# A graph-network kernel: the PE's signals in weighted, maximum and convolution passes moved from matmuls to one drain per unit

## What is computed

```
msg = relu(h_in[src] + edge_attr @ We[l] + be[l])          # L0, five message layers
agg = segment_sum(msg, dst)
...
agg = segment_sum(x[src] * edge_weight, dst)               # L1, the weighted pass
...
amax = segment_max(leaky_relu(a_src[src] + a_dst[dst]), dst)   # L2, the maximum pass
out  = segment_sum(h[src] * exp(alpha - amax) / denom, dst)    # L2, the attend pass
...
h = segment_sum(h[src] * norm, dst)                        # L3, three convolution passes
```

## Time and profile before

| | us |
|---|---|
| median of 3 runs | 10497.17 |
| lowest, highest | 10493.28, 10524.75 |
| the profiled execution | 10512.7 |
| its span, from the first to the last instruction | 10510.6 |

### The profile page before, as it was taken

The page is one execution under the profiler, slowest core; times in us unless marked ns, Lnnn a source line. Parts: engine busy times, 40 slices in busy tenths (PEclk is TensorE's granted clock), DMA queues, the critical chain, the costliest instruction groups (busy, mean ns, idle before and its releaser), DMA issues. The chain is left out here.

```text
span 10510.6 us, 129336 instructions
## 1 busy us (share of the span) xinstructions
PE 6092.0 (58%) x27369; PEld 4863.8 (46%) x27370; DVE 4112.3 (39%) x9347; ACT 1787.8 (17%) x5309; POOL 5218.2 (50%) x5246
## 2 busy tenths in 40 slices
PE   3567666765675666667456533457854564455454
PEld 2456545644563555456334423345633443344343
DVE  5344434444453444434312523337761223224123
ACT  3222222222222222222323210001210000000000
POOL 2654454445446545644565445530036655655655
PEclk9788877877887888778778865558977787788777
DMA  5332332333233323323322145423313222222322
GB/s 149 108 94 86 98 102 84 98 90 103 83 93 103 96 85 98 105 84 89 92 82 79 32 138 165 148 97 131 114 60 88 83 71 86 85 80 72 87 78 70
DMA packets 423906, 995.27 MB, mean 95 GB/s; under 512 B 124608, under 2 KB 190016, under 8 KB 407360
## 3 DMA queue, kind: packets, MB, share of 16 engines
q0 software_dynamic: 246800, 677.71, 22.4%
q1 hardware_dynamic: 152608, 293.79, 8.5%
q10 hardware_dynamic: 24336, 22.16, 0.6%
HBM read 858.93 MB, written 134.35 MB: 95 GB/s over the span
## 5 line engine op out<-in xcount | busy, mean ns | idle before, releaser
L283 POOL DMA_INDIRECT ring<-node_table,idx x4608 | 4510.2, 979 | 3679.3 <-issue 1667.8
L250 DVE SCALAR_TENSOR_TENSOR S<-iota,block_start,dst_f 128x512 f32<-128x512 f32 x1900 | 1423.2, 749 | 3256.2 <-remote 1813.2
L497 PE MATMUL psAT<-ring,S 128*128 128x256 f32 x7600 | 2023.4, 426 | 1065.6 <-DVE AGG L614 917.8
L321 PE MATMUL psAT<-ring,S 128*128 128x256 f32 x6080 | 1709.1, 443 | 1506.2 <-DVE AGG L365 743.3
L497 PEld LDWEIGHTS psAT<-ring,S 128*128 128x128 f32 x7600 | 1599.8, 216 | 1424.0 <-DVE S L250 759.9
L321 PEld LDWEIGHTS psAT<-ring,S 128*128 128x128 f32 x6080 | 1332.8, 225 | 1878.1 <-issue 1024.0
L656 DVE TENSOR_TENSOR ring<-ring,psE 128x256 f32<-128x256 f32 x2560 | 877.0, 416 | 744.7 <-remote 358.2
L566 ACT ACTIVATE ring<-ring 128x256 f32<-128x256 f32 x2560 | 841.9, 408 | 1235.0 <-issue 651.4
L283 POOL DMA_INDIRECT ring<-att_table,idx x512 | 492.6, 962 | 471.3 <-issue 471.3
L438 PE MATMUL psE<-we_stk,stk 128*128 128x256 bf16 x2560 | 428.5, 307 | 308.4 <-DVE ring L656 156.7
L750 PE MATMUL psAT<-shared,S 128*128 128x9 f32 x1520 | 340.1, 363 | 393.1 <-DVE shared L796 310.6
(11 more groups left out here) (304 smaller groups left out, 4772.8 us busy)
## 6 DMA issues: line engine op xcount, KB each, us to landing
stk<-stack_table SPq DMA_DIRECT2D x320, 256.0 KB
ring<-node_table,idx POOLq DMA_INDIRECT x4608
rows_table<-ring SPq DMA_DIRECT2D x64, 1072.0 KB
ring<-rows_table SPq DMA_DIRECT2D x64, 1072.0 KB, 4.9
node_table<-tab ACTq DMA_DIRECT2D x136, 128.0 KB
stack_table<-stk SPq DMA_DIRECT2D x64, 256.0 KB, 2.0
node_table<-tab SPq DMA_DIRECT2D x96, 128.0 KB, 1.7
ring<-att_table,idx POOLq DMA_INDIRECT x512
```

What stands on the lines that cost most here:

```text
L250: nc.vector.scalar_tensor_tensor(S[:, 4 * g:4 * g + 4, :], iota[:, :].unsqueeze(1).to_broadcast([P, 4, P]), block_start[:, bass.ds(blk, 1) ...
L283: nc.gpsimd.indirect_dma_start(ring[:, q, 0:gw], None, table, bass.IndirectOffsetOnAxis(ap=idx[:, q:q + 1], axis=0)).then_inc(gathered[q], 16)
L321: ins = nc.tensor.matmul(psA[:, 0:D], S[:, u, :], ring[:, q, 0:D], start=(u == 0), stop=(u == U - 1))
L497: ins = nc.tensor.matmul(psA[:, 0:D], S[:, u, :], ring[:, U * ob + u, 0:D], start=(u == 0), stop=(u == U - 1))
```

## The change

In `edge_pass`, `max_pass` and the side work of the weighted pass no matmul or transpose carries a signal any more. After the 8 matmuls of a unit the PE drains, and the drain adds 8 to `onehot_used`. The drain at the end of an octet goes, and `octet_free` is raised by a plain semaphore instruction. In `max_pass` a drain signals `scoresT` and another one `runsT`. The start of the weighted pass (`turn_weights`) and its side work do the same. `message_pass`, `attend_pass` and the node phases stay as they were.

```diff
@@ edge_pass, the unit
-                                    ins = nc.tensor.matmul(psA[:, 0:D], S[:, u, :], ring[:, q, 0:D],
-                                                           start=(u == 0), stop=(u == U - 1))
-                                    if u % 4 == 3:
-                                        ins.then_inc(onehot_used, 4)
+                                    nc.tensor.matmul(psA[:, 0:D], S[:, u, :], ring[:, q, 0:D],
+                                                     start=(u == 0), stop=(u == U - 1))
+                                pe.drain().then_inc(onehot_used, U)
                                 pe.reg_add(npe, npe, U)
 
                             units(pe, None, cnt, unit)
-                            pe.drain().then_inc(octet_free, 1)
+                            pe.sem_inc(octet_free, 1)
@@ max_pass
-                            nc.tensor.transpose(psE[:, 512:512 + P], d16[:, :], ident[:, :]).then_inc(scoresT, 1)
+                            nc.tensor.transpose(psE[:, 512:512 + P], d16[:, :], ident[:, :])
+                            pe.drain().then_inc(scoresT, 1)
...
-                            nc.tensor.transpose(psE[:, 1536:1536 + P], last[:, :], ident[:, :]).then_inc(runsT, 1)
+                            nc.tensor.transpose(psE[:, 1536:1536 + P], last[:, :], ident[:, :])
+                            pe.drain().then_inc(runsT, 1)
...
-                                        if u % 4 == 3:
-                                            ins.then_inc(onehot_used, 4)
+                                    pe.drain().then_inc(onehot_used, U)
@@ turn_weights, root_pe
-            ins.then_inc(weights_turned, 1)
+            pe.drain().then_inc(weights_turned, 1)
...
-                ins.then_inc(root_turned, 1)
+                pe.drain().then_inc(root_turned, 1)
...
-                ins.then_inc(root_done, 1)
+                pe.drain().then_inc(root_done, 1)
```

More of the change, by code:

```diff
@@ L749, in unit @@
                                             pe.wait_ge(onehot_ready, c + u + 4)
-                                        ins = nc.tensor.matmul(psA[:, (HEADS + 1) * u:(HEADS + 1) * (u + 1)],
-                                                               S[:, u, :], picks[:, U * half + u, :],
-                                                               start=True, stop=True)
-                                        if u % 4 == 3:
-                                            ins.then_inc(onehot_used, 4)
+                                        nc.tensor.matmul(psA[:, (HEADS + 1) * u:(HEADS + 1) * (u + 1)],
+                                                         S[:, u, :], picks[:, U * half + u, :],
+                                                         start=True, stop=True)
+                                    pe.drain().then_inc(onehot_used, U)
                                     pe.reg_add(npe, npe, U)
@@ L1851, in turn_weights @@
                     for g in range(2):
-                        ins = nc.tensor.transpose(turned_weight(s_, f)[:, P * g:P * g + P],
-                                                  w1_sb[:, g, D * s_ + P * f:D * s_ + P * f + P], ident[:, :])
-            ins.then_inc(weights_turned, 1)
+                        nc.tensor.transpose(turned_weight(s_, f)[:, P * g:P * g + P],
+                                            w1_sb[:, g, D * s_ + P * f:D * s_ + P * f + P], ident[:, :])
+            pe.drain().then_inc(weights_turned, 1)
         def copy_weights(dve):
@@ L1878, in root_pe @@
                     for f in range(2):
-                        ins = nc.tensor.transpose(psT[:, D * q + P * f:D * q + P * f + P],
-                                                  tin[:, q, P * f:P * f + P], ident[:, :])
-                ins.then_inc(root_turned, 1)
+                        nc.tensor.transpose(psT[:, D * q + P * f:D * q + P * f + P],
+                                            tin[:, q, P * f:P * f + P], ident[:, :])
+                pe.drain().then_inc(root_turned, 1)
             if ob == 2:
@@ L1887, in root_pe @@
                     for f in range(2):
-                        ins = nc.tensor.matmul(psO[:, D * q:D * q + D], tT[:, q, P * f:P * f + P], wb_sb[:, f, :],
-                                               start=(f == 0), stop=(f == 1))
-                ins.then_inc(root_done, 1)
+                        nc.tensor.matmul(psO[:, D * q:D * q + D], tT[:, q, P * f:P * f + P], wb_sb[:, f, :],
+                                         start=(f == 0), stop=(f == 1))
+                pe.drain().then_inc(root_done, 1)
         def root_act(act, i, ob):
```

## The result

| | before | after |
|---|---|---|
| median of 4 runs, taken together, us | 10510.96 | 10633.86 |
| lowest, highest | 10493.28, 10528.30 | 10602.67, 10670.11 |
| span of the profiled execution | 10510.6 | 10668.0 |
| mean granted TensorE clock | 0.783 | 0.783 |

The ratio is 1.0122, with a 95% interval of 1.0085 to 1.0159. A repeat on another chip, `change_again`, gave 1.0108 (1.0073 to 1.0142).

A forecast was written before the change was run, and what follows sets the result against it. It took POOL's gather stream, interrupted by PE's late signals, to bound the passes. Gains of 457 + 40 + 235 = 732 us from 10512.7 gave 9780.7, or 9770 as median; range 9600 to 10,700, for its own case 9600 to 10,000.

The forecast's parts named there:

- I take the first: PE's drains: lateness taken at its lower bound, the shortest old drain, 0.22 us in all.
- it is signals on matmuls that queue for a passage: PE's signals during POOL's gathers: they pass one at a time, and the old drain was late standing behind one.
- The upper bound: PE's drains: a drain is as late as the matmul signals are in the old kernel.
- 732 us of gain: Whole kernel: 457 from POOL's waits in edge passes, 40 at pass ends, 235 in the maximum pass.
- The stretch of the earlier trace that I gave as proof: Convolution pass: two pending signals came 6 us apart, the octet's drain at once after; POOL resumed 0.7 us after DVE.
- POOL's own stop lets them through: Passes with gathers: PE's signals arrive late while POOL streams gathers and get through when POOL stands still.
- not touched: Message layers, where POOL waits 996 us, the attend pass and node phases: left out of the gain.
- POOL's floor: Passes with gathers: 512 gathers at 1.25 us cannot take less than 640 us.
- rival 1: Edge and maximum passes: drains as late as signals, nothing gained, later one-hots added; 10,650 to 10,750 us, chance 0.27.
- The later one-hot: DVE's first half of S moves behind the unit's last matmul: +0.75 us per unit, +0.4 between octets, +0.9 in maximum pass.
- they come out during DVE's 1.3 us of one-hot and add: PE's branch and waits behind a unit's drain in edge passes: hidden by DVE's work, so no cost.
- The swap of the octet's drain: Octet's end in edge passes: a semaphore instruction replaces the drain at the same place, costed at nothing.

The follow-up runs named there:

- wait_landing: Kernel before, but POOL waits after each octet for its last gather to land, in weighted, maximum and convolution passes; 10402.62 us, ratio 0.9918.
- edge_drain: Kernel before with the change in the weighted and three convolution passes alone; 10582.66 us, ratio 1.0066.
- bare_drain: Kernel before, both signals kept, plus a drain that carries nothing behind each unit of the edge and maximum passes; 10591.93 us, ratio 1.0076.
- one_signal: Kernel before with a unit's two signals merged onto its 8th matmul in edge and maximum passes, no drain added; 10559.02 us, ratio 1.0051.
- max_drain: Kernel before with the drain per unit in the maximum pass alone, scoresT and runsT still signalled on matmuls; 10579.53 us, ratio 1.0067.
- drain_and_landing: Changed kernel, but POOL waits after each octet for its last gather to land, in weighted, maximum and convolution passes; 10389.72 us, ratio 0.9906.

## Why the prediction was wrong

**The step that failed** is "I take the first", the choice of the lower bound for a drain's lateness, with its reason, "it is signals on matmuls that queue for a passage". The upper bound was the true value: drains without a signal ahead of them took up to 33.6 and 40.2 us. All of the 732 us of gain hung on it. The stretch of the earlier trace rows that I gave as proof bears the other reading as well: if matmuls retire in order and late, the drain always follows right after the last one, however it was held. It could not tell the two apart, and I let it weigh against the old drains, which were often late (107 of 256). The 6 us between two signals were no queue either: in the stretch at 6499 us of the same trace, shown above, three signals that were held come out within 0.13 us. The Trainium skill (PSUM — Partial Sum Buffer, "Engine vs sequencer instructions") says that a drain waits until the engine is fully idle. These traces agree: each of the changed kernel's 475 unit drains ends behind its unit's last matmul record, by 0.02 to 38.2 us.

**What held.** On a chip with holds POOL's stream is what goes with the lateness, and a full stop after each octet removes it: `wait_landing` shows it. That "POOL's own stop lets them through" is true of most long holds, not of all (83 of 92, above). The message layers kept their length, but "not touched" hid that they lose most: with the stops everywhere a layer falls from 963 to 983 us to 851 to 868. That POOL's floor bounds the passes once PE is prompt was also right: 656 to 674 us for 512 gathers without holds, where I had computed 640.

**The terms of rival 1.** The later one-hot was priced at 0.75 within an octet and at most 0.4 at its end; the medians are 0.66 and 0.37, and the edge passes lost 90 us in the trace and 73 in `edge_drain`, against 93. The maximum pass was priced at 63 x 0.9 = 57; it measured 59 in the unit matmuls. That both sums came out near the measured ones, with a wrong make-up, is luck. I costed PE's sequencer behind the drain at nothing, "they come out during DVE's 1.3 us of one-hot and add", and the step to the next pair not at all. `bare_drain` measured +82 for that, and `one_signal` +50 for what I thought was all. The cover is there only within an octet; at the end of an octet the drain now stands ahead of the loop's branch (+0.37 in `bare_drain`), and before the next pair it keeps PE from running ahead (+1.08). On the other side the late one-hot costs less than priced; my explanation, which no run tests, is that a unit that is held loses nothing by it.

**The swap of the octet's drain** for a plain increment "at nothing" took the octet's end alone; the drain that stands there now, ahead of the loop's branch, is the +0.37 above. The side work's drains cost nothing visible: the weighted pass takes 1097.6 us without them in `edge_drain`, 1117.8 and 1097.4 with them in the two traces of the changed kernel.

**What stays open.** Why the weighted pass loses 37 to 57 us, and what a convolution pass loses: against the one trace before, `edge_drain` and the changed kernel have 4 to 24 us more in each, `change_again` has 6 and 7 more and once 17 less, and in `max_drain`, where these passes are untouched, they move by +2, -14 and -4, so single passes do not resolve it; what ends a hold while POOL goes on; why some chips hold PE's matmuls and others do not; and by what path POOL's gathers do it.

## What to carry to other kernels

A drain is no way around a late signal: it waits for the same completions, takes away the early signal halfway, and stops the engine's sequencer from running ahead; move work to a drain only where nothing stands behind it. Before you cost a remedy, ask whether the trace separates the causes that it could be for, and give a row that fits both no weight for either. And where a wait depends on what another engine issues, measure on several chips: pausing POOL's gathers gained 6.5% on a chip with holds and lost 19% on one without.

## What the runs showed of the hardware

- The same kernel before took 10,499 to 10,669 us on four chips and 8,253 to 8,263 on two. The mean granted clock is 0.78 of full speed on the one kind and 0.85 on the other; the gathers follow at 1.25 us on both.
- On the first kind matmuls retire up to 38 us after their modelled end while POOL issues indirect DMAs, even with a stop of 1.5 us per octet and one gather in flight, and next to never when POOL lets each octet land: 256 of 256 octet drains within 0.05 us in `wait_landing`, 2 of 380 unit drains over 0.3 us in the edge passes of `drain_and_landing`, and there 21 of the 159 drains of the maximum pass, by 1.9 us at most.
- A drain on POOL behind four gathers left 2.7 us between gathers in the middle of an octet and 3.0 at its end; waiting for the last to land left 2.7.
- The clock in the maximum pass is 0.50 of full speed, and a unit's 16 records take 3.58 us there at a prompt pace; no run changed it.
